# A macaron of two mixtures: shared products of the narrow stages moved ahead of the tiles, one of them into a routing pause

## What is computed

```python
x = x + 0.5 * ffn0(layernorm(x))       # 8 experts, hidden 176, shared hidden 352   stage 0
x = x + hgrn(layernorm(x))             # gated recurrence                            stage 1
x = x + 0.5 * ffn0(layernorm(x))                                                   # stage 2
x = x + 0.5 * ffn1(layernorm(x))       # 16 experts, hidden 128, shared hidden 128  stage 3
x = x + attention(layernorm(x))        # 4 heads of 64                               stage 4
x = x + 0.5 * ffn1(layernorm(x))                                                   # stage 5

def ffn1(x):
    scores = sigmoid(x @ gate_w)
    _, selected = top_k(scores + expert_bias, 2)
    top = scores at selected, divided by their sum
    shared = silu(x @ shared_gate_w) * (x @ shared_up_w) @ shared_down_w
    routed = sum over the 2 selected of top * (silu(g) * u @ experts_down[e])
    return shared + routed
```

## Time and profile before

| What | Value |
|---|---|
| Three executions | 876.32, 876.4 and 879.66 us, median 876.4 |
| The profiled execution | 874.5 us, its span 872.7 us |
| Granted TensorE clock, mean | 0.959 of full speed |
| TensorE busy | 775.0 us (89%), 3982 matmul records |
| VectorE busy | 501.5 us (57%) |
| ScalarE busy | 419.9 us (48%) |
| GpSimd busy | 299.5 us (34%) |
| Transfers | 135.26 MB, mean 155 GB/s |

### The profile page before, as it was taken

How to read it: one execution, slowest core, us unless ns; L and a number is a source line. 1 busy time by engine, 2 the same in 40 slices (tenths; PEclk the granted TensorE clock), 3 DMA queues, 4 the chain that set the end, 5 groups by cost and what they waited for, 6 DMA issues and landing times.

```text
span 872.7 us, 14545 instructions
## 1 busy us (share of the span) xinstructions
PE 775.0 (89%) x3982; PEld 552.1 (63%) x3982; DVE 501.5 (57%) x1737; ACT 419.9 (48%) x1020; POOL 299.5 (34%) x316
## 2 busy tenths in 40 slices
PE   5999999989898999999973899998899885999991
PEld 2446777754465446777752478887677663578881
DVE  4566332368857656323369662237898866662247
ACT  3822334317743812333336345553788777245550
POOL 0571433300000570443406717551011133617560
PEclk9999999999999999999985799999999998899996
DMA  8843333189999723333186245536000011245528
GB/s 294 260 151 109 114 103 100 55 273 371 342 344 344 247 103 108 110 109 97 55 309 258 104 127 180 154 107 213 1 1 2 1 50 48 89 140 178 157 100 292
DMA packets 102364, 135.26 MB, mean 155 GB/s; under 512 B 11366, under 2 KB 90726, under 8 KB 101734
## 3 DMA queue, kind: packets, MB, share of 16 engines
q1 hardware_dynamic: 87894, 95.05, 33.8%
q0 software_dynamic: 14400, 39.34, 12.7%
HBM read 56.23 MB, written 78.12 MB: 154 GB/s over the span
## 4 chain that ended last, share of the span: by engine, by line
PE 66%; DVE 17%; ACT 6%; issue 4%; DMA 3%; POOL 2%; SPq 1%; DVEq 0%; POOLq 0%; ACTq 0%
PE bank L1004 19%; PE bank L1025 12%; PE bank L898 10%; PE bank L984 4%; PE bank L1015 3%; PE bank L911 3%; PE bank L1070 2%; DVE X L1298 2%; DVE X L1302 2%; PE bank L838 2%; DVE st L1316 2%; PE bank L1121 2%; POOL slot_rows L508 2%; PE bank L1189 1%; DMA Y<-f_result_rows 1%
## 5 line engine op out<-in xcount | busy, mean ns | idle before, releaser
L508 POOL DMA_INDIRECT f_result_rows<-arena x172 | 164.9, 958 | 225.1 <-ACT arena L661 124.0
L508 POOL DMA_INDIRECT slot_rows<-XN,slots x128 | 123.8, 967 | 238.6 <-DVE slots L1427 179.3
L1004 PE MATMUL bank<-w,arena 128*128 x688 | 202.6, 417 | 0.7 <-ACT arena L648 0.7
L1628 DVE COPY arena<-bank 88x128 f32<-88x128 f32 (+1 forms) x250 | 65.2, 285 | 213.7 <-PE bank L1015 213.5
L1004 PEld LDWEIGHTS bank<-w,arena 128*128 128x128 f32 x688 | 129.3, 190 | 31.4 <-issue 1.6
L1025 PE MATMUL bank<-w,arena 88*128 (+1 forms) x500 | 136.5, 381 | 0.0
L898 PE MATMUL bank<-XT,f_s 128*128 128x512 f32 (+1 forms) x256 | 117.6, 607 | 2.8 <-DMA f_s<-in_f_s 1.2
L655 ACT ACTIVATE arena<-bank 128x128 f32<-128x128 f32 (+1 forms) x172 | 50.8, 295 | 116.6 <-PE bank L1004 116.6
L661 ACT ACTIVATE arena<-bank 128x256 f32<-128x256 f32 x172 | 65.9, 383 | 73.3 <-PE bank L1025 72.6
L1025 PEld LDWEIGHTS bank<-w,arena 88*128 88x128 f32 (+1 forms) x500 | 81.4, 190 | 5.6 <-issue 0.8
L898 PEld LDWEIGHTS bank<-XT,f_s 128*128 128x128 f32 (+1 forms) x256 | 46.0, 187 | 57.6 <-issue 53.3
(11 more groups left out here) (165 smaller groups left out, 1097.7 us busy)
## 6 DMA issues: line engine op xcount, KB each, us to landing
slot_rows<-zeros SPq DMA_DIRECT2D x16, 2176.0 KB, 18.0
arena<-slot_rows SPq DMA_DIRECT2D x172, 128.0 KB, 2.1
XN<-f_result_rows SPq DMA_DIRECT2D x32, 256.0 KB, 5.5
Y<-f_result_rows SPq DMA_DIRECT2D x32, 256.0 KB, 6.1
w<-in_f_w SPq DMA_DIRECT2D x1, 4096.0 KB, 16.2
w<-in_f_w SPq DMA_DIRECT2D x1, 2816.0 KB
f_result_rows<-arena POOLq DMA_INDIRECT x172, 2.6
X<-in_x SPq DMA_DIRECT2D x4, 512.0 KB, 5.8
```

The costliest lines, as they stand in the source:

```text
L508: pool.indirect_dma_start(out=dst, out_offset=bass.IndirectOffsetOnAxis(ap=idx, axis=0), in_=src, in_offset=None).then_inc(done.sem, 16)
L1004: last = pe.matmul(bank[2 + q % 2][:, 0:2 * m.H], xsT[q % 2][:, k, :], L["w13"][:, k, bass.ds(e, 1), :], start=(k == 0), stop=(k == KD - 1))
L1628: last = dve.tensor_copy(hT[q % 2][0:kp, k, :], bank[4 + q % 2][0:kp, k * P:(k + 1) * P])
```

## The change

In the narrow stages the first shared product of group 0 moves ahead of the last `positions`, in place of 22 of the 26 filler transposes. `HELD["f1"]` becomes 2: the second products of groups 0 and 1, and their eight additions, move from behind the tiles to ahead of them. The 16 filler transposes ahead of the tiles become 4. The hidden products of VectorE move so that each stands where its first product is now done: the first one ahead of the tile lists, the second ahead of `close_slots`, the third behind `copy_lists`. Behind the tiles, groups 2 and 3 are left for TensorE, and for VectorE group 2 (group 3 is added in the next stage's program, or at the end, as before). No function is new. The whole diff:

```diff
--- before.py
+++ after.py
@@ -373,7 +373,7 @@
 
         MAP_STEP = 5
         map_bank = bank[4 + (MAP_STEP - 1) % 2]
-        HELD = {"f0": 2, "f1": 0}
+        HELD = {"f0": 2, "f1": 2}
         HELD_UP = {len(MOE0.KS): 11, len(MOE1.KS): NG}
 
         def down_bank(s, g, half):
@@ -954,7 +954,8 @@
                     else:
                         logits_back(s, g)
                     if nk == 1 and g == NG - 1:
-                        keep_busy(26, 0)
+                        shared_up(0)
+                        keep_busy(4, 0)
                     if nk == 1:
                         positions(s, g)
                 if nk > 1:
@@ -968,12 +969,14 @@
                     shared_up(2 * NG + 2)
                     shared_down(1)
                 else:
-                    shared_up(0)
                     shared_up(1)
+                    shared_up(2)
                     tile_lists()
-                    shared_up(2)
                     shared_up(3)
-                    keep_busy(16, 0)
+                    pe.wait_ge(*s["experts"](1))
+                    shared_down(0)
+                    shared_down(1)
+                    keep_busy(4, 0)
 
 
                 def xT(j, q, r):
@@ -1594,6 +1597,8 @@
                                 finish(g + 1)
                             place(g)
                 place(NG - 1)
+                if nk == 1:
+                    shared_hidden(0, 1)
                 tile_lists()
                 if nk > 1:
                     shared_hidden(2 * NG, 2 * NG + 1)
@@ -1604,12 +1609,14 @@
                     shared_hidden(2 * NG + 1, 2 * NG + 3)
                     shared_add(s, 1)
                 else:
-                    shared_hidden(0, 1)
+                    shared_hidden(1, 2)
                     close_slots()
                     split_slots()
-                    shared_hidden(1, 2)
                     copy_lists()
-                    shared_hidden(2, NG)
+                    shared_hidden(2, 3)
+                    shared_add(s, 0)
+                    shared_hidden(3, NG)
+                    shared_add(s, 1)
                 dve.wait_ge(*s["rows_out"](16 * 2 * NTT))
                 mark(0, 0, NTT)
```

## The result

The changed kernel takes 879.59 us as the median of 20 executions (876.55 to 883.70), the kernel before 876.38 us in 20 beside them (872.77 to 879.66). The forecast was 881.6 us, with 876.0 to 886.0 as its range, and slower by over 0.5% a shade ahead of within 0.5%. Sign and range held; the size was too large by 2 us, and of the two cases that were all but level (0.47 and 0.46) the second came, within 0.5%. That the range held says little: the 876.4 us of the kernel before lay in it too.

A forecast was written before the change was run, and what follows sets the result against it. The prediction took VectorE's marks to set the tile loops' starts and transfers their ends. Starts of 0.4 and 0.9, ends of 0 and 3.9 for the gap after stage 3 gave +5.2 us: 881.6 us, range 876.0 to 886.0.

The forecast's parts named there:

- What bounds the start of the loops: Tile loops, stages 3 and 5: VectorE's mark sets the start; eight more additions move it +0.4 and +0.9 us.
- The product in the pause: Last choice pause: first product delays the counts +0.45 us in stage 3, +1.05 in stage 5, up to 1.7 more.
- Scatters: Row scatters before the loops: floor moves by 0.35 to 0.45 us in stage 3, nothing moves in stage 5.
- Ends of the loops at nothing: Behind the tiles, stages 3 and 5: transfers set both ends, so removed products and additions gain 0 (stage 5 bound -0.6).
- The gap after stage 3: Attention's start: TensorE idles 4.5 us, the clock falls, transposes, queries and keys run at half rate: +3.9 us (2.2 to 6).
- The sum: Whole kernel: 0.4 + 0.9 + 0 + 3.9 = +5.2 us, against the median 881.6 us.
- The clock-holds rival: Gap after stage 3: the clock holds, only the loop starts count, +1.3 us, 877.7 us; chance 0.20.
- The earlier start: Tile loops: additions fit VectorE's waits, marks start at the floor, -2.8 us with loop end, 873.6 us; chance 0.10.
- The 0.07 for faster: Whole kernel: chance given to a faster result, beside 0.47 for slower and 0.46 for same.
- rival 3: Attention's start: values and scores suffer from the low clock too, +6.5 us there, +7.8 in all, 884.2 us; chance 0.05.
- rival 4: Choice pauses: counts delayed by the whole half-rate time, marks 2.1 and 2.6 us later, clock falls, +8.6, 885.0 us; chance 0.05.
- The rule of thumb of the Trainium skill: Gap after stage 3: half of some 12 us throttled would be 6 us there, sum 7.3; prediction did not take it whole.

The follow-up runs named there:

- Experiment 3: Changed kernel with the pause's 26 fillers and first-product order as before, second products still ahead of the tiles: 886.84 us against 876.19 for the kernel before.
- experiment 5: Changed kernel with one group's second product and additions ahead of the tiles instead of two, plus 28 fillers: 877.58 us against 876.86 for the kernel before.
- experiment 4: Changed kernel with HELD back at 0, keeping the first product in the pause, 44 fillers ahead of the tiles: 876.47 us against 876.19 for the kernel before.
- experiment 6: Kernel before with 46 instead of 36 fillers at the attention's start and 6 and 8 more in two later waits: 876.46 us against 876.86.
- experiment 1: Changed kernel with 68 instead of 36 filler transposes at the attention's start: 878.97 us against 876.19 for the kernel before, ratio 1.0016.
- experiment 8: Unaltered programs profiled again, kernel before once and changed kernel twice: single executions of 878.84 us, and 881.43 and 881.10 us.
- experiment 9: Kernel before with half a first product and 6 fillers in the pause, HELD at 0, 32 fillers ahead of tiles: 874.82 us against 876.48; repeated, ratio 0.9984.
- experiment 2: Kernel before with 4 instead of 36 filler transposes at the attention's start, nothing else: 876.66 us against 876.19, ratio 1.0002.
- experiment 7: Kernel of experiment 4 with first products 0 and 1 in the last two choice pauses, 24 fillers in earlier ones: 880.77 us against 876.86 for the kernel before.

## Why the prediction was right, and where it was not

**What bounds the start of the loops** was read rightly. VectorE's mark does, and stepping through the two queues with eight additions ahead of it gave about the right place. Over the profiles, from the first counts to the first tile, the changed kernel took 51.56, 50.66 and 51.19 us, the kernel before 50.47 and 50.64: about +0.6 where +0.4 stood. In stage 5, from group 2's counts, it was 29.34, 29.08 and 29.14 against 28.26 and 28.71: about +0.7 where +0.9 stood. Experiment 3 shows the price of the second products and additions without the pause (3.5 and 3.6 us against 3.3), and experiment 5 that one group fewer gives back 1.2 us in stage 3.

The two halves of the change nearly cancel behind the counts. From the last counts to the first tile the kernel before took 19.53 us and the changed one 19.29, in each of their profiles within 0.02, and in stage 5 as well as in stage 3 (there 28.26 less 8.74, and 29.34 less 10.05). So what the starts lose is the lateness of the counts and no more: the first product in the pause makes room behind the counts for the work that was moved there, and pays for it by delaying them.

**The product in the pause** costs what the term said where the clock rises as early as in the first profile of the kernel before, 28.8 us behind the first counts of stage 3: the counts were 0.45 us late in experiment 4 and 0.43 in the changed kernel's second profile. In its other two the clock rose 29.8 and 30.6 us behind them, and the counts came 0.95 and 1.33 us late. The prediction named that case and put a bound of 1.7 on it.

**Scatters:** held. In stage 3 the row loads moved with the counts, in stage 5 the queue hid them.

**Ends of the loops at nothing:** held in stage 3, where VectorE's wait for the result rows grew from 1.88 to 5.10 us and the first addition of result rows stood 10.4 to 10.5 us behind the last hidden product in all profiles of both kernels. In stage 5 the first pair started 0.5 us sooner, and no gain is seen at the end: from the last tile to the end the five profiles with two groups held took 26.71 to 27.87 us (mean 27.2), the eight with none held 26.65 to 28.53 (mean 27.5). The 0.7 us by which the changed kernel's three lie above the two of the kernel before are within that scatter: experiment 6, which is the kernel before at this place, took 28.53.

**The gap after stage 3: +3.9 us. This is the step that failed.** TensorE idled 4.5 to 4.7 us and the clock did fall, in every profile with the gap. Two parts of the term were wrong. First, it took the baseline for a kernel whose clock holds. That was true of the one profile shown; in others, of this kernel and of versions without the gap, the clock falls at the same place, in the thin work behind the first transposes (experiments 1, 4, 8 and 9). Second, it put transposes, queries and keys all at half rate. In the changed kernel's first profile and in experiments 2 and 3 the keys ran at 1.00 again; in its second and third both were slow (3.78 us each). The price of a fall itself was near, if a little below. Combine to row maxima took 16.28 or 16.29 us in the three profiles whose clock held there (the first of the kernel before, experiment 6, the second of experiment 9), 17.3 to 18.3 where the queries alone were slow, and 19.1 to 20.0 where the keys were slow too: 1.0 to 2.0 and 2.8 to 3.7 us more, where 2.2 and 3.9 stood. What the gap adds is only the difference in how often and how long the clock is down. The five profiles with the gap (the changed kernel's three, experiments 2 and 3) took 17.72 to 19.96 us (mean 18.8; the one-held version, with a shorter gap, had 19.55), those of the kernel before, the filled changed kernel, and experiments 4 and 9 took 16.28 to 19.07. Against the kernel before alone (mean 17.7) that is +1.1 us, with a spread as large; experiment 2 gives +0.5 from its median, experiment 1 up to 1.8. So the term is 0.5 to 1.8 us, not 3.9, and below its lower bound for a fallen clock (2.2), since the fall is in the baseline as well.

**The sum.** 0.6 + 0.7 at the starts and 0.5 to 1.8 behind the gap make 1.8 to 3.1 us against the 3.2 measured. The starts are shown; the gap's share is known only within that range, and what is left, 0.1 to 1.4 us, stays open. The attention's end (experiment 8) is a place where some of it may lie.

**The rivals.** The clock-holds rival had the wrong mechanism and a time (877.7) below the measured one by 1.9 us. The earlier start did not come: the additions did not fit into VectorE's waits, because they stand behind second products that stand behind all first ones. (The 0.07 for faster does not follow from its chance either, since its own time, 873.6, lies within 0.5%.) Of rival 3, the values ran slow for a part in the second and third profile (2.32 and 2.56 us for eight records instead of 1.89), which is 0.4 to 0.7 us and not 1.7. Of rival 4, the late counts came in part (1.33 and 1.31 us in the first profile), and its 885.0 us lies above all twenty executions.

The rule of thumb of the Trainium skill (TensorE: Matmul & The Clock Gate, Terms), half of the throttled time as penalty, would have given an estimate of 3.4 us for the 6.8 us at 0.50 of the changed kernel's first profile. Against the profiles whose clock held, that profile lost 1.4 us there, and the third, with 13.6 us at 0.50, lost 3.7. Both are less than half of the time at 0.50, so the measurement decides against taking the rule whole here.

## What to carry to other kernels

Before work is moved from behind a loop to ahead of it, read at both ends who waits: here the work stood under a transfer behind the loop, where it cost nothing, and VectorE's idle time ahead of the loop lay before the moved work was ready for it. Alone, that move cost 3.5 us at each start (experiment 3). A move that depends on another one to make room for it is best measured with each half alone. Here neither half paid by itself (experiments 3 and 4); what probably did was half a first product in the pause, which left the counts where they were (experiment 9). One profile is one case of where the clock fell: a term that rests on a clock that held in it needs a second profile of the same kernel.

## What was not expected of the hardware

The time of one program goes with how long its clock is granted 0.50. Over the 20 executions of the changed kernel the mean granted clock ran from 0.945 (883.70 us) to 0.952 (877.32, 877.28 and 876.89 us). The same binary spreads by 7 us, twice the effect that was studied. At the end of the program the low rate costs nothing: the changed kernel stands at 0.50 for its last 18.9 us and the kernel before for its last 14.2 (first profiles), both after the last matmul. And more fillers do not fix it by themselves: in experiment 7 the mean clock of the profile was 0.971, the highest of all, and the kernel 4 us slower than before.
